# Deformable convolutions on TensorE: samples moved between the two distance products, 64x64 weighted tiles, copied offset rows, and a smaller patch in the second convolution

## What is computed

```
off = conv2d(x, w_off, b_off)            # 18 numbers for each pixel: dy, dx of 9 taps
ys = row - 2 + 2*ky + dy ; xs = col - 2 + 2*kx + dx
sampled[tap] = bilinear(x, ys, xs)       # zero outside of the image
out = einsum('oik,bikhw->bohw', w_dc, sampled)
```

## Time and profile before

| | |
|---|---|
| median of 3 runs | 966.86 us (961.87 to 967.53) |
| profiled execution | 967.68 us, of which the span of instructions is 965.7 us |
| mean granted TensorE clock | 0.90 of full |
| busy shares of the span | TensorE 77%, VectorE 56%, ScalarE 47%, GpSimd 17% |
| loop of the first convolution | 51.6 to 263.3 us |
| loop of the second convolution | 305.8 to 577.1 us |

### The profile page before, as it was taken

The page is one execution under the profiler, slowest core; times in us unless marked ns, Lnnn a source line. Parts: engine busy times, 40 slices in busy tenths (PEclk is TensorE's granted clock), DMA queues, the critical chain, the costliest instruction groups (busy, mean ns, idle before and its releaser), DMA issues.

```text
span 965.7 us, 39200 instructions
## 1 busy us (share of the span) xinstructions
PE 744.0 (77%) x17378; PEld 563.6 (58%) x17378; DVE 538.7 (56%) x993; ACT 452.1 (47%) x750; POOL 166.6 (17%) x200
## 2 busy tenths in 40 slices
PE   6477777777685676676676676699999999999546
PEld 2255555555423454354354345589999999999434
DVE  2465666656534445445455456346666666666843
ACT  1355556565634544444353453335554444454441
POOL 4000000000000000000000003244444444443210
PEclk8789999999997977888887896789999999999779
DMA  8400000000022000000000006100000000000002
GB/s 208 89 4 1 0 1 0 0 1 0 2 41 37 5 3 5 5 4 5 4 4 4 4 5 157 45 1 2 1 0 0 0 0 0 0 0 0 1 0 89
DMA packets 8146, 17.56 MB, mean 18 GB/s; under 512 B 2149, under 2 KB 6117, under 8 KB 7605
## 3 DMA queue, kind: packets, MB, share of 16 engines
q1 hardware_dynamic: 8022, 15.74, 6.6%
HBM read 11.87 MB, written 3.87 MB: 16 GB/s over the span
## 4 chain that ended last, share of the span: by engine, by line
PE 65%; ACT 13%; DVE 9%; issue 8%; DMA 3%; POOL 1%; SPq 1%; ACTq 0%; DVEq 0%
PE banks L214 13%; PE banks L111 9%; ACT y L238 7%; PE banks L778 7%; PE banks L762 6%; PE banks L808 6%; PE banks L149 5%; PE banks L548 4%; PE banks L819 3%; DVE s L327 3%; PE banks L798 3%; ACT hy L256 2%; PE banks L773 2%; PE banks L195 2%; PE banks L130 2%
## 5 line engine op out<-in xcount | busy, mean ns | idle before, releaser
L214 PE MATMUL banks<-s,y 32*64 32x96 f32 (+2 forms) x9216 | 155.6, 262 | 20.0 <-DVE s L327 16.9
L214 PEld LDWEIGHTS banks<-s,y 32*64 32x64 f32 x9216 | 130.2, 141 | 65.0 <-DVE s L327 39.1
L238 ACT COPY y<-banks 128x768 f32<-128x768 f32 x106 | 84.4, 800 | 153.3 <-PE banks L111 153.3
L327 DVE TENSOR_TENSOR s<-hy,y 128x384 f32<-128x384 f32 x288 | 146.8, 552 | 0.1
L312 DVE TENSOR_SCALAR y<-y 128x384 f32<-128x384 f32 x144 | 51.7, 359 | 150.9 <-ACT y L247 150.8
L149 PE MATMUL banks<-off,near_sel 128*128 (+1 forms) x296 | 63.2, 299 | 75.5 <-ACT y L238 64.8
L247 ACT ACTIVATE y<-banks 128x384 f32<-128x384 f32 x160 | 78.3, 493 | 78.6 <-PE banks L130 77.7
L256 ACT ACTIVATE hy<-banks,row_bias 128x512 f32<-128x512 f32 x148 | 101.6, 686 | 22.1 <-PE banks L149 22.0
L374 POOL COPY stage<-src 128x128 f32<-128x128 f32 x72 | 18.9, 306 | 497.0 <-PE banks L111 497.0
L111 PE MATMUL banks<-w_dc,stage 64*32 64x192 f32 x3392 | 98.5, 343 | 4.5 <-ACT y L238 4.5
L130 PE MATMUL banks<-off,near_sel 128*128 (+2 forms) x640 | 60.7, 225 | 48.5 <-issue 28.4
(11 more groups left out here) (147 smaller groups left out, 1015.7 us busy)
## 6 DMA issues: line engine op xcount, KB each, us to landing
src<-in_x_dram SPq DMA_DIRECT2D x4, 578.0 KB, 5.8
y<-in_w_dram SPq DMA_DIRECT2D x1, 2080.0 KB
off<-in_w_dram SPq DMA_DIRECT2D x2, 1024.0 KB
out_dram<-tokens SPq DMA_DIRECT2D x4, 512.0 KB, 2.6
offsets_dram<-tokens SPq DMA_DIRECT2D x32, 54.0 KB
off<-offsets_dram SPq DMA_DIRECT2D x16, 108.0 KB
near_sel<-in_near_sel_dram SPq DMA_DIRECT2D x1, 960.0 KB
w_dc<-in_w_dc_dram SPq DMA_DIRECT2D x2, 288.0 KB, 10.3
```

What stands on the lines that cost most here:

```text
L214: last = nc.tensor.matmul(out[:, r0:r0 + n, first:first + width], m.yk[32 * j:32 * j + 32, ky, g, col, kx * C:(kx + 1) * C], s_rows(m, cv, ...
L238: nc.scalar.copy(m.yk[:, ky, :, 2 * part:2 * part + 2, :].rearrange("p g a n -> p g (a n)"), slot_banks(m, k)[:, :, 0:384]).then_inc(cv.em ...
L327: nc.vector.tensor_tensor(dst.rearrange("p r g (a c) -> p (r g) a c", a=TC), y, x.rearrange("p r g (a c) -> p (r g) a c", a=TC), ALU.mult) ...
```

## The change

1. In TensorE's step, samples now stand between x and y: before x, y, samples, w; now x, samples, y, w. In a weighted step, y also waits until x has been emptied.
2. A weighted item takes two images at once: stationary tiles of 64 rows by 64 columns, 8 matmuls where there were 16. `IMAGES` and the layout of `stage` follow.
3. The distance matmuls no longer read the large offset buffer through an address that depends on the loop's register, with all 128 rows. GpSimd copies the rows that a tap needs into `near_off` (9 slots, one for each tap), and the matmuls read 20 rows at a fixed place. The copy of tap t in tile row i waits until y of the same tap in row i-1 is done; TensorE waits for it with `off_near`.
4. The waits of the near path for both offset halves move from TensorE to GpSimd: the first copy waits for half 0, the second half is waited for where a copy first needs it. ScalarE waits before it first overwrites the parts.
5. The second convolution's reach is 1: its patches have 6x10 outputs where they had 8x12.

```diff
-REACHES = [2, 2]
+REACHES = [2, 1]
-IMAGES = [[0, 1, 2, 3], [5, 4, 7, 6]]
+IMAGES = [[0, 2, 1, 3], [5, 7, 4, 6]]
...
     for col in (2 * part, 2 * part + 1):
-        for j in range(4):
+        for half in range(2):
             for g in range(2):
-                image = IMAGES[g][j]
+                image = IMAGES[g][2 * half]
                 rows = slice(C * (image % 2), C * (image % 2) + C)
                 last = nc.tensor.matmul(
-                    m.ps[32 * j:32 * j + 32, ...],
-                    m.stage[rows, image // 2, col, :], cv.w_dc[rows, 3 * ky:3 * ky + 3, :],
+                    m.ps[C * half:C * half + C, ...],
+                    m.stage[rows, col, 2 * g:2 * g + 2, :].rearrange("p a n -> p (a n)"),
...
 def sampler_pe(nc, pe, m, cv):
     old = 2 * cv.reach
-    for half in range(HALVES):
-        pe.wait_ge(cv.moved[half], MOVES)
...
             pe.wait_ge(cv.emptied, i * PER_ROW + (k - 1))
-            columns_near(nc, m, cv, k, tap, new_rows(cv, tap) + TILE_ROWS * later, TILE_ROWS, i)
-            k += 1
-            pe.wait_ge(cv.emptied, i * PER_ROW + (k - 1))
-            rows_near(nc, m, cv, k, tap, first_row(cv, tap) + TILE_ROWS * later, i)
+            pe.wait_ge(cv.off_near, i * TAPS + (t + AHEAD + 1))
+            columns_near(nc, m, cv, k, tap, old, TILE_ROWS)
             k += 1
...
             last.then_inc(cv.sampled, 1)
+            pe.wait_ge(cv.emptied, i * PER_ROW + (k - 1))
+            if t in STEP_WEIGHTED:
+
+                pe.wait_ge(cv.emptied, i * PER_ROW + k)
+                if STEP_WEIGHTED[t] == (0, 0, 1):
+                    pe.wait_ge(cv.staged, i * PAIRS + 2 * PAIRS)
+            rows_near(nc, m, cv, k, tap)
+            k += 1
             if t in STEP_WEIGHTED:
                 weighted_near(nc, m, cv, k, *STEP_WEIGHTED[t][0:2])
                 k += 1
...
 def sampler_pool(nc, pool, m, cv):
...
+    for n in range(TR * TAPS + AHEAD):
+        tile_row, tap = divmod(n, TAPS)
+        if tile_row:
+            pool.wait_ge(cv.filled, EMPTIED_AT["y", tap, tile_row - 1])
...
+        if moved == 0 or moved == 1 and row + rows >= HALF_ROWS:
+            pool.wait_ge(cv.moved[moved], MOVES)
+            moved += 1
...
+        nc.gpsimd.tensor_copy(m.near_off[:, tap, left_out:size], m.off_flat[:, at + left_out:at + size]
+                              ).then_inc(cv.off_near, 1)
```

More of the change, by code:

```diff
@@ L123, in columns_near, with rows_near @@
         wide = 2 * cv.reach if late else TILE_COLS
-        first = tap * PIX + row * W + ahead - 2 * kx + TILE_COLS * late
+        first = MARGIN + row * W + ahead - 2 * kx + TILE_COLS * late
         for g in range(2):
-            src = m.off_flat[:, first:first + n * W] if i is None else tile_rows(m.off_flat, first, n, i)
-            src = src.rearrange("p (r c w) -> p r c w", c=TC, w=TILE_COLS) if i is None else src.rearrange(
-                "p r (c w) -> p r c w", c=TC)
+            part = group_rows(g, 1)
+            src = m.near_off[part, tap, first:first + n * W].rearrange("p (r c w) -> p r c w", c=TC, w=TILE_COLS)
             dst = slot_banks(m, k)[:, g, 0:n * TC * cols].rearrange("p (r c w) -> p r c w", c=TC, w=cols)
             last = nc.tensor.matmul(dst[:, :, :, TILE_COLS * late:TILE_COLS * late + wide],
-                                    m.near_sel[:, 6 + ((ahead * 3 + kx) * 2 + late) * 2 + g, :], src[:, :, :, 0:wide],
+                                    m.near_sel[part, 3 + (ahead * 3 + kx) * 2 + late, :], src[:, :, :, 0:wide],
                                     start=True, stop=True, skip_group_check=True)
     last.then_inc(cv.filled, 1)
[L136 to L142, removed]
+def rows_near(nc, m, cv, k, tap):
     n = window(cv)[0]
-    first = tap * PIX + row * W
     for g in range(2):
[L147 to L150, removed]
+        part = group_rows(g, 0)
+        last = nc.tensor.matmul(slot_banks(m, k)[:, g, 0:n * W], m.near_sel[part, tap // 3, :],
+                                m.near_off[part, tap, MARGIN:MARGIN + n * W], start=True, stop=True,
+                                skip_group_check=True)
     last.then_inc(cv.filled, 1)
@@ L293, in sampler_act @@
                 if t == TAPS - 1 and kind == "w" and tile_row < TR - 1:
+                    if tile_row == 0:
+                        for half in range(HALVES):
+                            for g in range(2):
+                                act.wait_ge(cv.bounced[half][g], 64)
                     act.wait_ge(cv.sampled, TAPS * (tile_row + 1))
@@ L364, in sampler_pool @@
 def sampler_pool(nc, pool, m, cv):
-    for tile_row in range(1, TR + 1):
-        pool.wait_ge(cv.filled, EMPTIED_AT["w", 2, 1, tile_row - 1])
-        stage_pool(nc, m, cv, min(tile_row, TR - 1))
+    rows = window(cv)[0]
+    moved = 0
+    for n in range(TR * TAPS + AHEAD):
+        tile_row, tap = divmod(n, TAPS)
+        if tile_row:
+            pool.wait_ge(cv.filled, EMPTIED_AT["y", tap, tile_row - 1])
+        row = TILE_ROWS * tile_row + first_row(cv, tap)
+        first = row * W - MARGIN
+        left_out = max(-first, 0)
+        if moved == 0 or moved == 1 and row + rows >= HALF_ROWS:
+            pool.wait_ge(cv.moved[moved], MOVES)
+            moved += 1
+        at = OFF_HEAD + tap * PIX + first
+        size = rows * W + 2 * MARGIN
+        nc.gpsimd.tensor_copy(m.near_off[:, tap, left_out:size], m.off_flat[:, at + left_out:at + size]
+                              ).then_inc(cv.off_near, 1)
+        if tap == AHEAD - 1 and tile_row:
+            pool.wait_ge(cv.filled, EMPTIED_AT["w", 2, 1, tile_row - 1])
+            stage_pool(nc, m, cv, min(tile_row, TR - 1))
 def stage_pool(nc, m, cv, tile_row):
```

65 lines of the change are left out of this document (32 added, 33 removed).

## The result

The changed kernel takes 995.81 us (median of 4 runs, 995.72 to 998.63), the one before 967.19 in its runs of that time. The ratio is 1.032, 95% interval 1.028 to 1.037: slower. The profiled execution took 995.72 us with a span of 993.7. The granted clock over the span fell from 0.90 to 0.757.

What follows compares the result with a forecast made beforehand. Chains of waits between engines, not busy time, were taken to bound the loops. 967.68 us, +39 for the loops (281 + 241 - 483.0) and -13 for the prologues gave 994 us, 2.8% slower; range 943 to 1030.

Steps and rivals of the forecast that it cites:

- The chain: Both loops: each samples waits through y, ScalarE, hat and s for the samples before; 3.45 us a step, 2.90 in second.
- the short y: Chain's link from y to ScalarE: about 0.33 us for 0.42 if y's two 20-row matmuls run beside each other.
- The clock: Both loops: falls once a tile row in steps without w, returns in weighted ones; loops 257 to 281, 226 to 241 us.
- nearly unbroken work brings it back: Weighted steps: TensorE's own work, as long as the step at low clock, brings the full clock back.
- The row at 584.50: Profile row of the kernel before: TensorE busy 1.72 of 3.40 us, then clock 0.50; taken as evidence that steps without w lose it.
- stream the same columns: Distance matmuls: 20 rows instead of 128 stream the same columns, x stays at 0.34 us.
- 64x64 tiles: Weighted items: w takes 0.85 to 0.88 us beside the chain, nothing in time.
- Fetches: Second loop's returns: the shorter loop ends seven stalls of 4.23 + 1.07 us, 37 us, and the slow work behind them.
- third rival: Second loop still refetched at each return: 37 us more than forecast, 1031 us; chance 0.07.
- Copied rows: GpSimd's 74 copies a convolution, 0.3 to 0.55 us each, have 25 us of cover: nothing in the loop.
- Offset waits: Ahead of both loops: shorter waits for offsets save 6.8 and 6.1 us, together -13, bounds -8 to -15.
- Rival 1: Clock never falls in the changed loops: 257 and 226 us, 955 us in all, faster than before; chance 0.18.

Runs made afterwards that it cites:

- experiment 4: Changed kernel plus 16 filler matmuls of zeros in each of the steps t = 1, 2, 3: 994.05 us, ratio 1.019 to the kernel before.
- experiment 3: Changed kernel with VectorE making s of a step ahead of the next step's hats: 886.66 us, ratio 0.911 to the kernel before.
- experiment 1: Changed kernel with only TensorE's old order put back (y ahead of samples): 955.65 us, ratio 0.982 to the kernel before.
- experiment 6: Changed kernel with TensorE's old order and distance matmuls reading all 128 rows: 898.37 us, ratio 0.921 to the kernel before.
- experiment 5: Kernel before with the 64x64 weighted tiles alone: 917.46 us, ratio 0.940 to the kernel before.
- experiment 8: Kernel of experiment 7 with the old 64x32 weighted tiles: 904.15 us, ratio 0.929 to the kernel before.
- experiment 7: Changed kernel with VectorE's s ahead of the next hats and 128-row distance matmuls: 844.53 us, ratio 0.869 to the kernel before.
- experiment 9: Kernel before with 96 small instructions ahead of the second convolution's loop, which moves its place: 924.00 us, ratio 0.954.
- the square: Four kernels crossing y ahead of or behind samples with 128 or 20 rows: 898.4 and 990.2 us at 128, 955.7 and 995.8 at 20.
- experiment 10: Changed kernel, new order kept, with 128-row distance matmuls alone: 990.18 us, ratio 1.022 to the kernel before.
- experiment 11: Kernel of experiment 7 with reach 2 in the second convolution too: 859.65 us, ratio 0.888 to the kernel before.
- experiment 2: Kernel before with TensorE's new order alone (y behind samples): 1080.61 us, ratio 1.108 to the kernel before.

## Why the prediction came out right, and where its steps were wrong

The time (994 forecast, 995.8 measured) and the sign came out right. The two loops were forecast at 281 and 241 us and took 274.2 and 249.0; the parts are these.

- **The chain** (3.48 in sum, 3.45 taken, 3.39 with the short y): measured 3.39 at full clock and 3.99 at the lower in the first convolution (forecast 4.0 to 4.2); 2.79 in the second at full clock (experiment 4), for 2.90. That VectorE's order is its other end is shown by experiment 3, which removes it with TensorE's program untouched. Right.
- **The clock.** The forecast had the steps without w as its only cause, a return in each tile row, and so half of the first loop low. The first loop did that: in the tile row shown the clock was low from 157.5 to about 173 us, came back in the weighted steps, and fell again near 190. The mean of 0.51 says that the second loop was low for nearly all of its time. The step that failed is "nearly unbroken work brings it back": in the second loop (rows at 463 and 469) and in experiment 3 work was nearly unbroken and the clock stayed at 0.50. The row at 584.50, from which the forecast had its idea of too little work, was also weak ground: TensorE's 1.72 us stand in one piece at its end, behind 2.19 us of waiting (`586.18 1.21 PE L1663 MATMUL banks<-y 64*64 64x64 f32 x32 [2.19 <-DMA y<-in_w_attn_dram]`), and not spread over it as in a step. The prediction said of 20 rows in place of 128 that they "stream the same columns", and costed them at nothing. Experiments 1 and 6 differ in those rows alone: 57 us. The second loop's 249.0 for 241 hides two errors that nearly cancel. By the forecast's own prices a loop that is low throughout would take 24 x 3.15 + 48 x 4.1 + 17 = 289 us; but a low weighted step took 3.23, not 4.1, since that price was added up from the kernel before, with its larger patches and 128-row distances.
- **What that does to the sum.** With the old order the 20 rows cost 57 us, with the new one 6, which is within the scatter between series; the order costs 92 us at 128 rows and 40 at 20. At a low clock the waits of the chain are filled by slower work (the weighted step of 3.23 us has no wait left), so each cause hides a good part of the other. My sum came near because it charged both loops for a low clock, on a reason that held only in part; for the second loop that is luck.
- **64x64 tiles, nothing in time**: right (experiment 5's first loop, experiment 8's against 7's).
- **Fetches**: right that they end, 52 to 57 us at a high clock (experiments 5 and 8), where 37 and the slow work behind them were named. Experiment 9 shows that the place of the loop in the program is enough, since neither length nor content changed. In the changed kernel most of that gain was lost again: the second loop fell by 21.6 only. The third rival did not come, and the sentence of the Trainium skill ("Runtime: NRT & Kernel Launch", Instruction fetch mechanics) by which every return would stall doesn't hold for these loops: they returned without a stall after the change and in experiment 9. Which places stall exactly was not mapped.
- **Copied rows**: hidden, as said; 0.38 us each, and TensorE waits for them at the start only.
- **Offset waits**: forecast -13 with bounds of -8 to -15, measured -16.7 ahead of the loops. The waits themselves were sized well: the first distance matmul runs 7.1 us earlier in the first convolution (37.52 for 44.66) and 5.0 earlier, counted from the end of the loop ahead, in the second, 12.1 together. The other 4.6 lie between the first distance matmul and the loop, a stretch that became shorter (5.2 for 7.0 us, and 4.2 for 6.9) and for which the sum had no term.
- **Behind the loops** the kernel lost 3.0 us that no term had. No instruction changed there. In the first 18.6 us behind the loops the clock was 0.68 where it had been 0.81, which may be a part of it; I did not follow it up.
- **Rival 1** (the clock never falls) was the live question, and the square answers it in part: even with 128 rows the new order lets the clock fall, to 0.82 and 0.79, and the time is 990. Its 955 could not be reached that way. (Its low bounds add up to 942 us, where the range was given from 943.)

## What to carry to other kernels

Before moving an instruction on one engine, write down the other engines' fixed orders and look for a cycle: here VectorE's "hats of the next step first" made a harmless swap into a chain of 3.4 us, and changing that one place turned a loss of 3% into a gain of 9% (13% with the wide distance matmuls). Treat a change of a matmul's array rows as a possible change of the clock, and compare the granted clock of the two kernels before explaining a slow loop by its waits. A long loop that stands in "issue" at its returns while an instruction queue is at work is worth a test at another place in the program before anything in it is tuned.

## What the runs showed of the hardware

- TensorE at work for 28.67 of 30 us and the clock at 0.50 throughout (experiment 3), with samples of 32 rows, w of 64 and distances of 20. With 128-row distances, which add no instructions and no columns, the same kernel had 0.90 over that loop (experiment 7) for 0.56. Busy time alone did not restore the clock in these runs; reading 128 rows in place of 20 did most of it, in matmuls that are 53 of the 162 us that the engine is busy in that loop. The 20-row matmuls also run beside each other (y to ScalarE 0.32 us for 0.42; y and the next x start 0.01 us apart at 155.06 in the changed kernel, and 0.23 apart at 225.28 with 128 rows in experiment 10), so that fewer rows and less time with columns passing came together; the runs do not separate these.
- With the same 20-row distances the clock came back in the weighted steps of the changed kernel's first loop (near 173 and near 205 us), with its 8x12 patches, and not in the second, with 6x10. With 128 rows the smaller patch costs 0.04 of clock (0.90 for 0.94, experiments 7 and 11); how much of the second loop's 0.51 it is was not tested.
- The Trainium skill ("TensorE: Matmul & The Clock Gate", Part 1) says that activity releases the clock and idleness takes it back. The falls in the first loops of experiments 2 and 10 agree only if steps full of waits count as idleness: the longest stretch there without a matmul was 2.01 us. Experiment 3 does not agree, if activity is read as time at work.
- An identical loop of 1717 instructions stalled some 4 us at each return at one place in the program and not 96 instructions further on (experiment 9), a difference of 51 us in a loop of 271.
- w with 16 records on 64x64 tiles takes the 0.88 us that 32 records on 64x32 take.
